# A gated cross-attention and mixture-of-experts layer on one core: the router's products on four column quarters, its running counts inside PSUM, the bias row added in place, and the steps of each group in another order

## The chip, the cores and the metric

One core of a Trainium2 chip runs the whole program in one launch. The time is the device time of one execution, in microseconds (us); lower is better. The engines are TensorE (PE, with its weight loads as PEld), VectorE (DVE), ScalarE (ACT), GpSimd (POOL) and SyncE (SP, which issues DMAs).

## What is computed

Four sequences of 1024 tokens with 256 features. The text side is normalised and attends over its context (64 rows of 192 features, masked) and over itself; the result, gated, is added to the tokens. Then each token goes to two of eight experts.

```python
x = x + tanh(g_xattn) * xattn(ctx, layernorm(x), mask)   # 4 heads of 64, keys: 64 context rows + 1024 own rows
...
    qn = rmsnorm(q, qn_g) * SCALE;  kn = rmsnorm(k, kn_g)
    attn = softmax(where(mask, qn @ kn.T, -max));  out = (attn @ v) @ Wo.T + bo
...
y = layernorm(x)
logits = y @ w_router;  probs = softmax(logits);  topk_w, topk_idx = top_k(probs, 2)
x = x + tanh(g_ffn) * sum_over_chosen(weight * (gelu(y @ w1[e] + b1[e]) @ w2[e] + b2[e]))
```

## The kernel before

**Two parts.** The first part does the attention, the second normalisation and the routing, and scatters each token's row twice (once for each chosen expert) into a table in HBM. The second part (`experts_phase`) walks over tiles of 256 rows of that table, one expert's weights at a time; it starts when all rows are scattered.

**Windows and groups.** The attention is cut into 8 windows `w` (sequence `b = w // 2`, pair of heads `w % 2`). A window has 18 units `u`, 2 query halves by 9 key tiles (8 of own rows, the ninth the context's), taken two at a time in 9 groups, `i` = 0 to 8. A group is written out by hand for each engine, as a list of steps in a fixed order:

- TensorE: `scores` of two units (K and Q, three products each for two heads), `tile_steps` (two transposes `turn_heads` of the tile projected in the group before, then `project` of the next tile), `values` of the first unit of the group before, the `mid_uses`, `values` of its second unit, `sums` (every ninth unit: the softmax's denominators), and the `late_uses`. With `i == 5` the `tile_steps` stand behind the first `values`.
- ScalarE: `probabilities` of the two units (exp from PSUM), `heads_hi`, `read_projection`, then whatever belongs to another stage: `norm_hi`, `norm_rows`, `normed_rows`, `turned_rows`, `second_rows`, `take_values`.
- VectorE: `add_probabilities` (adds the exps of nine units), `heads_lo`, `mean_squares`, `add_probabilities`, `scale_heads`, and what belongs to other stages: `quotients` (i 1 and 6), `residual`, `second_stats`, `second_variance`, `norm_lo`, `norm_stats`, `router_*`.
- GpSimd: `head_roots` (the power -1/2 for the head norms), `norm_root`, `second_root`, and the indirect DMAs of `scatter`.

A tile goes round all of them: `project` (PE), `read_projection` (ACT), `mean_squares` (DVE), `head_roots` (POOL), `scale_heads` (DVE), and `turn_heads` (PE) in the next group.

**The mid and late uses.** In an even window the projection of the sequence before (`project_out`, i 0 to 3; each of its two row tiles is two fp32 products and one product `bo_pick` by `bo_cut` that adds the bias row) and the transposes of the normed rows (`turn_rows`, i 7 and 8); in an odd window the transposes of the next sequence's normed rows (`turn_norm`, i 0 to 4), and `logits` (i 0) and `ranks` (i 4) of the sequence before. These results lie in the two PSUM banks `psF` that the projected tiles use in turn; `wait_bank_free` waits until the last user of a bank has been read. Behind the last window the same steps stand one after the other for the last sequence (`tail_uses`).

**The router.** `logits` is 16 products (8 row tiles by 2 halves of the features) of the turned rows as weights and the 128x8 router as moving data. `router_logits`, `router_softmax`, `router_largest` (twice) and `router_rows` on VectorE find the two experts; `ranks` multiplies the 0/1 matrix `chosen` by a triangular matrix and by ones; `router_slots` adds up the counts of the eight row tiles one after the other (`base`, eight small adds that wait for each other), and makes the row numbers for `scatter`.

## Time and profile before

| | us |
|---|---|
| median of 3 runs | 1027.05 (1022.74 to 1029.36) |
| profiled execution, its own time | 1023.27 |
| its span, first to last instruction | 1021.7 |
| attention, the eight windows | 43.9 to 517.4 |
| tail: last sequence's projection, norm, routing and scatter | 517.4 to 583.3 |
| experts | 583.3 to the end |
| granted TensorE clock, mean | 0.944 of full |

The profile is of one execution. A busy TensorE is an engine with an instruction in flight; at half clock it is busy too, for longer. [...]

### The profile page before, as it was taken

To read this page: it belongs to the slowest core of one execution; us is meant where nothing else is said; L and a number is where in the kernel's file an instruction comes from. 1 tells how busy PE (TensorE), PEld (TensorE's weight loads), DVE (VectorE), ACT (ScalarE), POOL (GpSimd) and SP (SyncE) were. 2 spreads that over 40 slices of the span, in tenths; PEclk is the share of its full clock that TensorE was granted. 3 is DMA by queue.
4 is the path that set the end of the run, shared out by engine and by line. 5 is a ranking of instruction groups with operands and counts; after the bars stand their busy time and mean duration, and the time that the engine had idled before them with its cause. 6 is when DMAs were issued, how large, how long until landed. Compare 5 with 4: busy or idle time off the path is not lost. (4 is left out here: it accounts for less than half of the span.)

```text
span 1021.7 us, 19903 instructions
## 1 busy us (share of the span) xinstructions
PE 890.3 (87%) x6028; PEld 682.5 (67%) x6028; DVE 625.9 (61%) x1497; ACT 544.4 (53%) x1439; POOL 351.8 (34%) x271
## 2 busy tenths in 40 slices
PE   4899989898898978989772099999999999999990
PEld 3644445454454645545342099999999999999990
DVE  5566676656766476564966156676757657757650
ACT  3777755856658566475513035454546445546430
POOL 2333232322655225552162422423323423333221
PEclk8999999998999899999995599999999999999996
DMA  4301000210002210010032342525252534342325
GB/s 124 126 1 44 2 0 20 68 40 2 32 32 67 79 42 32 32 63 1 16 110 71 107 129 41 134 45 130 44 136 41 134 46 129 54 126 42 50 32 174
DMA packets 49215, 66.31 MB, mean 65 GB/s; under 512 B 7409, under 2 KB 42993, under 8 KB 49105
## 3 DMA queue, kind: packets, MB, share of 16 engines
q0 software_dynamic: 17520, 33.27, 14.8%
q1 hardware_dynamic: 29296, 30.18, 10.0%
q10 hardware_dynamic: 2352, 2.31, 0.8%
q8 instruction: 22, 0.36, 0.1%
q14 instruction: 25, 0.20, 0.1%
HBM read 41.54 MB, written 28.39 MB: 68 GB/s over the span
## 5 line engine op out<-in xcount | busy, mean ns | idle before, releaser
L500 POOL TENSOR_TENSOR rr<-ssm,minus_half 128x4 f32<-128x4 f32 (+1 forms) x72 | 121.7, 1690 | 290.5 <-DVE ssm L791 290.5
L1615 PE MATMUL psH<-xT_hi,Q 128*128 128x256 f32 x1120 | 203.9, 281 | 1.6 <-DVE xT_lo L1532 1.6
L1628 PE MATMUL psY<-K,g_hi 128*128 128x256 f32 x1120 | 203.4, 284 | 0.0
L1468 POOL DMA_INDIRECT total<-y_out,token_i x70 | 115.0, 1643 | 255.4 <-DVE y_out L1553 243.9
L665 ACT ACTIVATE p_ring<-psS,shift 128x1024 f32<-128x1024 f32 x128 | 137.1, 1111 | 104.2 <-PE psS L1263 104.1
L1615 PEld LDWEIGHTS psH<-xT_hi,Q 128*128 128x128 f32 x1120 | 174.5, 190 | 2.0 <-issue 2.0
L1628 PEld LDWEIGHTS psY<-K,g_hi 128*128 128x128 f32 x1120 | 171.7, 188 | 0.0
L1628 PE MATMUL psY<-K,g_lo 128*128 128x256 f32 x560 | 157.3, 281 | 0.0
L1615 PE MATMUL psH<-xT_lo,Q 128*128 128x256 f32 x560 | 157.2, 281 | 0.0
L1279 PE MATMUL psO<-p_ring,V 128*64 128x512 f32 x576 | 151.5, 623 | 0.8 <-ACT o_sb L653 0.8
L827 DVE TENSOR_TENSOR p_sum<-p_sum,p_ring 128x1024 f32<-128x1024 f32 (+1 forms) x112 | 136.5, 1219 | 2.2 <-ACT p_ring L665 1.4
L1502 ACT ACTIVATE g<-psH,b_col 128x256 f32<-128x256 f32 x280 | 113.8, 474 | 29.6 <-DVE g_lo L1569 28.0
L1502 ACT ACT_TABLE_LOAD x35 | 44.9, 1283 | 158.8 <-PE psH L1615 158.7
L1263 PE MATMUL psS<-Q,K 64*128 64x512 f32 x864 | 126.8, 427 | 0.5 <-ACT p_ring L665 0.5
L1263 PEld LDWEIGHTS psS<-Q,K 64*128 64x128 f32 x864 | 79.9, 195 | 63.6 <-issue 44.1
L1567 DVE CAST g_hi<-g 128x512 fp32r<-128x512 f32 x140 | 62.7, 448 | 77.1 <-ACT g L1502 77.1
L1615 PEld LDWEIGHTS psH<-xT_lo,Q 128*128 128x128 f32 x560 | 106.2, 190 | 0.0
L1628 PEld LDWEIGHTS psY<-K,g_lo 128*128 128x128 f32 x560 | 105.7, 189 | 0.0
L1569 DVE TENSOR_TENSOR g_lo<-g,g_hi 128x512 fp32r<-128x512 f32 x140 | 96.9, 692 | 4.8
L508 POOL DMA_INDIRECT routed<-big,slot_i x64 | 72.1, 1127 | 57.7 <-ACT big L615 20.6
L1547 DVE TENSOR_TENSOR y<-psY,b_row 128x256 f32<-128x256 f32 x70 | 29.0, 423 | 56.7 <-PE psY L1628 56.7
L1279 PEld LDWEIGHTS psO<-p_ring,V 128*64 128x64 f32 x576 | 32.0, 138 | 46.4 <-issue 38.2
(238 smaller groups left out, 1248.7 us busy)
## 6 DMA issues: line engine op xcount, KB each, us to landing
lnf<-routed SPq DMA_DIRECT2D x35, 258.0 KB
xr<-in_L_ffn_w POOLq DMA_DIRECT2D x7, 1024.0 KB, 6.3
xn<-in_L_ffn_w POOLq DMA_DIRECT2D x7, 1024.0 KB, 8.7
xr<-in_x SPq DMA_DIRECT2D x8, 512.0 KB, 4.8
xb<-in_x SPq DMA_DIRECT2D x4, 1024.0 KB, 6.2
total<-xb SPq DMA_DIRECT2D x4, 1024.0 KB, 4.5
routed<-pad_rows SPq DMA_DIRECT2D x8, 258.0 KB, 4.4
total<-y_out,token_i POOLq DMA_INDIRECT x70, 3.9
```

The costliest lines, as they stand in the source:

```text
L500: pool.tensor_tensor(rr[0:p, c % 2, n], ssm[0:p, c % 2, n], minus_half[0:p, n], ALU.pow).then_inc(rr_ready, 1)
L508: pool.indirect_dma_start(routed, bass.IndirectOffsetOnAxis(ap=slot_i[:, k, t:t + 1], axis=0), rows[k][:, t, :], None, bounds_check=NE * R ...
L665: act.activation(p_ring[0:p, u % RING, :], psS[u % 2][0:p].rearrange("p a n -> p (a n)"), ACT.Exp, bias=bias).then_inc(exp_done, 1)
L827: dve.tensor_tensor(total, p_ring[0:p, (u - 1) % RING, :] if k == 1 else total, p_ring[0:p, u % RING, :], ALU.add).then_inc(p_added, 1)
L1263: ins = pe.matmul(psS[u % 2][:, odd, :], kk[rows_of, f, keys], qq[rows_of, f, cols], start=(m == 0), stop=(m == len(products) - 1))
L1279: ins = pe.matmul(psO[0][head, :], V[:, (w % 2) * KT + kt, head], p_ring[:, u % RING, odd * HALF:(odd + 1) * HALF], start=(kt == 0), stop= ...
L1468: pool.indirect_dma_start(total, bass.IndirectOffsetOnAxis(ap=token_i[:, m:m + 1], axis=0), y_out[:, m, :], None, bounds_check=NTOK + TM - ...
L1502: act.activation(g32[:, q % 2, (c % 2) * TM:(c % 2 + 1) * TM], psH[q][:, (c % 2) * TM:(c % 2 + 1) * TM], ACT.Gelu_apprx_tanh, bias=b1_col[ ...
L1567: dve.tensor_copy(g_hi[:, 2 * q:2 * q + 2, :], g).then_inc(g_hi_ready, 1)
L1569: dve.tensor_tensor(g_lo[:, 2 * q:2 * q + 2, :], g, g_hi[:, 2 * q:2 * q + 2, :].bitcast(F32), ALU.subtract).then_inc(g_ready, 1)
L1615: ins = pe.matmul(o, l, r, start=(n == 0), stop=(n == len(parts) - 1))
L1628: ins = pe.matmul(psY[m][:, 0:D], l[:, c, cols], r[:, c, :], start=(c == 0 and n == 0), stop=(c == HC - 1 and n == 2))
```

## The change

- `router` becomes 32 columns wide (8 used, the rest zero) and is the weights of `logits`: for each half of the features, four products, each on a quarter of the array's columns, over 256 of the 1024 turned rows. The result (`lgT`, experts in partitions) is copied to SBUF by ScalarE (`take_logits`) and turned back by two transposes (`turn_logits`, use `lt`); VectorE reads the logits from there.
- `ranks` is one product with the triangular matrix over 72 columns and eight with the ones, over 64, 56, ... 8 columns, added in PSUM, so that each tile's prefix comes out of PSUM; `router_slots` needs one add for the slots and one for `base`, which begins at each expert's region.
- The bias row is no longer a product: `tbo`, the gated bias, is added to the residual rows in place (`residual_base`, two adds of 128x1024 in groups 7 and 8 of each even window).
- TensorE does both `values` and the `sums` before the mid uses. `turn_rows`' odd uses and two of the `lt` go to the bank of the sums (bank 7); the tail uses spread over six banks.
- Steps of other stages move: `logits` to i 1 (i 0 in the last window), `lt` one later, `ranks` to i 6 (i 4 in the last), the router's steps on VectorE and ScalarE with them; `norm_lo` ahead of `quotients`; `second_offsets` behind `scale_heads`; `norm_stats` and `norm_variance` into the odd window, `norm_root` to its group 8; `scatter` to i 7 and 8 of the odd window and i 0 to 5 of the even one (from i 6, and i 0 to 4), in the last window from i 5.

```diff
@@ uses of the banks
+                if w % 2 == 1 and b >= 1:
+                    last = b + 1 == B
+                    if i == (0 if last else 1):
+                        return [("logits", b - 1)]
+                    if i == (1 if last else 2):
+                        return [("lt", b - 1)]
+                    if i == (4 if last else 6):
+                        return [("ranks", b - 1)]
...
+                        apart = name[0] == "turn" or name[0] == "lt" and name[1] + 2 < B
+                        yield 7 if apart else g % 2, name
@@ GpSimd
-                        if b + 1 < B and i == (4 if b == 0 else 1):
-                            norm_root(b + 1)
+                        if b == 0 and i == 4:
+                            norm_root(1)
                         if b >= 1 and i == 5:
                             second_root(b - 1)
-                        if b >= 2 and i < 5:
-                            scatter(b - 2, 6 + 2 * i, 2)
+                        if b >= 2 and i < 6:
+                            scatter(b - 2, 4 + 2 * i, 2)
...
+                    if w % 2 == 1 and i == 8 and b + 2 < B:
+                        norm_root(b + 2)
@@ ScalarE
+                def take_logits(b):
+                    name = ("logits", b)
+                    act.wait_ge(logits_done, b + 1)
+                    act.activation(lgT[:], bank(name)[:, 0:2 * P], ACT.Copy).then_inc(bank_read[bank_of[name]], 1)
...
-                        first = 5 if b == 0 else 2
+                        first = 5 if b == 0 else 1
                         if first <= i < first + 4:
                             norm_rows(b + 1, 2 * (i - first), 2)
@@ VectorE
+                def residual_base(b, half):
+                    dve.wait_ge(xb_loaded[b % 2], b // 2 * 16 + 16)
...
+                    dve.tensor_tensor(xb[:, b % 2, t, :], xb[:, b % 2, t, :], tbo[:].unsqueeze(1).to_broadcast([P, HT, D]),
+                                      ALU.add).then_inc(xb_ready, 1)
...
-                    for t in range(T):
-                        dve.tensor_tensor(base[:, t + 1, :], base[:, t, :], bank(name)[:, D + t * NE:D + (t + 1) * NE],
-                                          ALU.add).then_inc(base_ready, 1)
-                        dve.wait_ge(base_ready, b * (T + 2) + (t + 1))
...
+                    then_step(dve.tensor_tensor(slot[:], bank(name)[:, 0:T * NE].rearrange("p (t e) -> p t e", t=T),
+                                                base[:].unsqueeze(1).to_broadcast([P, T, NE]), ALU.add))
+                    dve.tensor_tensor(base[:], base[:], bank(name)[:, T * NE:(T + 1) * NE],
                                       ALU.add).then_inc(bank_read[bank_of[name]], 1)
...
+                    if not even and past and i == (5 if last else 7):
+                        router_slots(b - 1)
+                    if not even and past and last and i == 3:
+                        router_softmax(b - 1)
+                    if not even and past and last and i == 4:
+                        router_largest(b - 1, 1)
+                        router_rows(b - 1)
...
+                    if not even and more and i < 5:
+                        norm_lo(b + 1, i)
+                    if even and past and i == 6:
+                        second_offsets(b - 1)
...
+                    if even and i in (7, 8):
+                        residual_base(b, i - 7)
...
+                        if i in ((2, 3) if b == 0 else (0, 2)):
+                            norm_stats(b + 2, i - 2 if b == 0 else i // 2)
+                        if i == 8:
+                            norm_variance(b + 2)
...
+                        if i == 4:
+                            router_softmax(b - 1)
+                            router_largest(b - 1, 0)
+                        if i == 5:
+                            router_largest(b - 1, 1)
                             router_rows(b - 1)
@@ TensorE
-                    for t in range(T):
-                        ins = passes(bank(name)[:, t * NE:(t + 1) * NE], [(yT[:, c, t * P:(t + 1) * P], router[:, c, :]) for c in range(EC)])
+                    for c in range(EC):
+                        for j in range(4):
+                            ins = pe.matmul(bank(name)[j * BLOCK:(j + 1) * BLOCK, 0:2 * P], router[:, c, :],
+                                            yT[:, c, j * 2 * P:(j + 1) * 2 * P], start=(c == 0), stop=(c == EC - 1))
...
-                    pe.matmul(bank(name)[:, 0:T * NE], tri[:], chosen[:], start=True, stop=True)
-                    pe.matmul(bank(name)[:, D:D + T * NE], ones[:], chosen[:], start=True, stop=True).then_inc(rank_done, 1)
+                    pe.matmul(bank(name)[:, 0:(T + 1) * NE], tri[:], chosen[:], start=True, stop=False)
+                    for t in range(T):
+                        behind = bank(name)[:, (t + 1) * NE:(T + 1) * NE].rearrange("p (t e) -> p t e", e=NE)
+                        ins = pe.matmul(behind, ones[:], chosen[:, t * NE:(t + 1) * NE].unsqueeze(1).to_broadcast([P, T - t, NE]),
+                                        start=False, stop=(t == T - 1))
...
-                                     + [(bo_pick[:], bo_cut[:])])
...
                         values(2 * g - 2)
+                        values(2 * g - 1)
                     if i == 5:
                         tile_steps(g)
+                    if g >= 1:
+                        for u in (2 * g - 2, 2 * g - 1):
+                            sums(u)
                     for name in mid_uses(w, i):
                         use(name)
-                    if g >= 1:
-                        values(2 * g - 1)
-                        for u in (2 * g - 2, 2 * g - 1):
-                            sums(u)
```

## Rows read from the trace of the kernel before

**Rows 1.** The page: TensorE's busy time, and its granted clock in 40 slices

```profile
PE 890.3 (87%) x6028; PEld 682.5 (67%) x6028; DVE 625.9 (61%) x1497; ACT 544.4 (53%) x1439; POOL 351.8 (34%) x271
...
PEclk8999999998999899999995599999999999999996
```

**Rows 2.** Busy time by stretch: windows 1, 3, 6, 7, tail, experts

```profile
core 0: us, PE busy (x) PEld busy (x) DVE busy (x) ACT busy (x) POOL busy (x), PEclk, DMA share, GB/s
...
88.50:145.00 56.50, 50.92 (x279) 26.57 (x279) 37.53 (x73) 39.73 (x127) 16.63 (x10) 0.97 0.07 20
...
208.30:274.70 66.40, 57.74 (x313) 32.12 (x311) 42.47 (x106) 42.10 (x129) 19.97 (x13) 0.92 0.03 9
...
404.40:468.10 63.70, 59.95 (x317) 32.61 (x317) 39.45 (x87) 38.65 (x126) 32.88 (x23) 1.00 0.12 42
468.10:517.40 49.30, 43.18 (x241) 22.01 (x241) 34.80 (x72) 24.91 (x42) 13.58 (x10) 0.93 0.05 19
517.40:583.30 65.90, 20.61 (x96) 14.68 (x92) 29.45 (x102) 8.92 (x12) 27.69 (x26) 0.64 0.34 103
583.30:1000.50 417.20, 413.28 (x3500) 412.72 (x3500) 266.35 (x596) 204.14 (x386) 134.63 (x97) 0.99 0.38 80
```

**Rows 3.** Waits of TensorE, 40 to 520 us (total, times, longest)

```profile
PE psF L1206 <- DVE qkd L801: 16.5, 16, 1.9
PE psF L1232 <- DVE chosen L929: 10.1, 3, 4.3
PE psF L1160 <- DVE ln_lo L786: 5.0, 3, 1.9
PE psF L1216 <- DVE K L812: 4.4, 3, 1.5
```

**Rows 4.** Timeline of TensorE, window 3: logits and the scores behind

```profile
214.23 3.74 PE L1160 MATMUL psF<-router,yT 128*128 128x8 f32 x32
217.90 2.57 PE L1263 MATMUL psS<-Q,K 64*128 64x512 f32 x12
```

**Rows 5.** Timeline of TensorE, window 4, group 0: the projection's products

```profile
278.78 1.13 PE L1160 MATMUL psF<-wo,att 128*128 128x256 f32 x4
279.84 0.38 PE L1160 MATMUL psF<-bo_cut,bo_pick 64*128 64x256 f32 x1
280.15 1.13 PE L1160 MATMUL psF<-wo,att 128*128 128x256 f32 x4
```

**Rows 6.** Timeline of TensorE, window 2, group 6: both value steps together

```profile
190.07 1.94 PE L1279 MATMUL psO<-p_ring,V 128*64 128x512 f32 x8
...
191.94 1.65 PE L1263 MATMUL psS<-Q,K 64*128 64x512 f32 x12
```

**Rows 7.** Timeline of window 2, groups 5 to 7: roots, offsets, next transposes

```profile
186.69 1.01 POOL L500 TENSOR_TENSOR rr<-ssm,minus_half 128x4 f32<-128x4 f32 x1 [3.62 <-DVE ssm L791]
...
188.99 2.55 POOL L495 TENSOR_TENSOR rstd<-var,minus_half 128x8 f32<-128x8 f32 x1 [1.29 <-DVE var L870]
...
191.77 2.08 ACT L609 ACTIVATE big<-xb,off,rstd 128x256 f32<-128x256 f32 x4 [0.17 <-DVE off L762]
...
192.35 1.91 POOL L500 TENSOR_TENSOR rr<-ssm,minus_half 128x4 f32<-128x4 f32 x1 [0.81 <-DVE ssm L791]
...
194.78 0.44 PE L1206 MATMUL psF<-ident,qkd 128*128 128x128 f32 x2 [1.19 <-DVE qkd L801]
```

**Rows 8.** GpSimd's indirect DMAs: ns shortest/median/longest

```profile
L508 POOL DMA_INDIRECT routed<-big,slot_i x64: 970/1024/1967, 263.3 to 575.1; - x64
```

**Rows 9.** VectorE's adds of 128x1024 by form, 30 to 530 us

```profile
L827 DVE TENSOR_TENSOR p_sum<-p_sum,p_ring 128x1024 f32<-128x1024 f32 x96 | 117.1, 1220 | 2.1 <-ACT p_ring L665 1.4
```

**Rows 10.** Timeline of the tail: logits, counts, last scatter

```profile
539.98 4.58 PE L1160 MATMUL psF<-router,yT 128*128 128x8 f32 x32 [0.78 <-ACT yT L641]
...
550.06 1.53 DVE L945 TENSOR_TENSOR base<-base,psF 128x8 f32<-128x8 f32 x8
...
575.10 0.97 POOL L508 DMA_INDIRECT routed<-big,slot_i  x1 [0.30 <-issue]
```

More of the change, by code:

```diff
@@ L1050, in _ @@
                         quotients(2 * w)
-                    if even and past and i < 4:
-                        residual(b - 1, i)
-                    if not even and more and i < 5:
-                        norm_lo(b + 1, i)
-                    if even and past and i == 5:
-                        second_variance(b - 1)
-                    if even and more:
-                        if i == 0 and b >= 1:
-                            norm_variance(b + 1)
-                        if i == 7:
-                            mask_to_bias(b + 1)
+                    if even and past:
+                        if i < 4:
+                            residual(b - 1, i)
+                        if 2 <= i < 6:
+                            second_stats(b - 1, i - 2)
+                        if i == 5:
+                            second_variance(b - 1)
+                    if even and i in (7, 8):
+                        residual_base(b, i - 7)
+                    if even and more and i == 7:
+                        mask_to_bias(b + 1)
                     if w == 0 and i in (1, 2):
@@ L1238, in project_out @@
                     pe.wait_ge(att_ready, b * 4 + (3 if q < 2 else 4))
[L1239 to L1240 removed]
                     for n in range(2):
                         t = 2 * q + n
[L1243 to L1244 removed]
+                        ins = passes(bank(name)[:, n * D:(n + 1) * D], [(att[:, c, t * P:(t + 1) * P], wo[:, c, :]) for c in range(EC)])
                     ins.then_inc(o_done, 1)
@@ L1288, in sums @@
                     pe.wait_ge(p_added, (j + 1) * (SUMS - 1))
-                    if j == 0:
-                        wait_bank_read(pe, ("tile", 5))
-                    if kt == SUMS - 1 and j > 0:
-                        pe.wait_ge(den_taken, u // KT)
+                    wait_bank_free(pe, ("sums", j))
                     for odd in range(2):
@@ L1298, in use @@
                 def use(name):
-                    kind = {"wo": turn_output_weights, "norm": turn_norm, "out": project_out, "turn": turn_rows, "logits": logits, "ranks": ranks}[name[0]]
+                    kind = {"wo": turn_output_weights, "norm": turn_norm, "out": project_out, "turn": turn_rows, "logits": logits, "lt": turn_logits,
+                            "ranks": ranks}[name[0]]
                     kind(*name[1:])
```

163 lines of the change are left out of this document (86 added, 77 removed).

## The prediction

> **What bounds the kernel now.** The page comes first: TensorE is busy for 890.3 of 1021.7 us, VectorE for 61%, the others less [rows 1]. So the question in each stage is why TensorE is not at work, or at work slowly. The view by stretch splits this [rows 2]. The experts (417 us) are TensorE work without gaps; nothing of the change touches them. The attention is 473.5 us: in window 3 TensorE is busy 57.74 of 66.40 us, 8.7 idle, in window 6 59.95 of 63.70, in window 7 43.18 of 49.30; windows 2 and 4 are like 6 (3.4 and 4.3 idle) and 5 like 3 (7.8). The tail (65.9 us) is a chain through all engines with TensorE busy a third of it.
>
> The granted clock is the second loss. [...] The timeline shows what went before: the twelve score products behind the logits take 2.57 us against 1.65 [rows 4, 6]. Behind 32 products of 8 columns the engine runs at half clock though it was never idle; other such stretches follow waits of 1.8 us and more.
>
> The waits say what the idle time is [rows 3]: 16.5 us for VectorE's `scale_heads` (the loop of a tile through ACT, DVE, POOL, DVE, which needs about 7.2 us from a group's first score to the next `turn_heads`, as long as a plain group of 4.9 us with the 1.6 us of scores behind it, and a little more), 10.1 for `chosen` ahead of `ranks`, 5.0 for `ln_lo`, 4.4 for a bank ahead of `turn_rows`.
>
> **The bias row.** In `project_out` the bo product adds 280.15 - 279.84 = 0.31 us to each row tile [rows 5]. 24 of them lie in the attention: -7.4 us; 8 in the tail, where TensorE sets the pace: -2.5. Part is given back: in group 1 of an even window VectorE does `quotients` (2.35 us) ahead of `residual`, and the project of group 2 needs that bank. Today the residual ends just in time; TensorE arriving 1.1 us sooner waits 1.1, three times, +3.3. The replacement is eight adds of 128x1024, 1.22 us each [rows 9], in groups 7 and 8 of even windows. VectorE has the room there on average; each pushes the next `mean_squares` some 0.7 us where the loop is tight. I take +0.5 for window 0 and have the rest in the sums by window below; without cover it is 9.8 us.
>
> **The logits.** 32 instructions take 217.90 - 214.23 = 3.67 us in window 3 [rows 4]. The new form is 16 instructions of 256 columns. No row has products on a quarter of the columns; the bounds are from the nearest. The projection, on all columns, takes 1.06 us for four instructions of 256 columns [rows 5], 4.2 for 16. The values, on halves of the columns, take 191.94 - 190.07 = 1.87 us for eight of 512 [rows 6]; for 16 of 256 that is 1.9, and if the quarters overlapped four deep it would be 0.9. I take 1.8, since the order on the engine (the two passes of one product, then of its neighbour) is that of the values. With two transposes (0.3) the sum is -1.6 for each sequence, -4.8 in the attention. [...]
>
> `ranks` grows from two small products to nine, about 0.06 to 0.1 us each: +0.5 a sequence, +1.5 in the attention.
>
> **Both value steps together.** Eight value instructions take 1.87 us together and about 2.05 when a mid use splits them, as the second column half of each step overlaps only with a value step. 34 groups have a mid use: 34 x 0.15 = -5 us. The mid use also comes 0.9 us later in its group, so the small bank waits (0.4 and 0.1) in the projections go.
>
> **The waits, window by window.** I followed each engine's list through a group with the durations of the trace (exps 2.0, heads 0.55, reads of a projection 1.05, a norm's pair on ACT 1.45, an add 1.14 pace, POOL's root 1.92).
> - Windows 3 and 5: the `ln_lo` wait (1.8, 1.2) goes, as `norm_lo` now stands ahead of `quotients`; the wait for `chosen` (2.9) with the bank wait before it (1.1) goes, as `ranks` stands two groups later. In their place: `logits` now stands directly behind `turn_norm` in the same bank and waits for ACT's two reads, 1.5. `router_softmax` and `router_largest` (3.8 us with `router_rows`) fall into groups 4 and 5, `quotients` into 6, `router_slots` to the top of 7: VectorE gets behind, `mean_squares` is late by 1 us in group 5, 1.6 in 6 and 2.8 in 7. And `project` of group 7 wants the bank that `router_slots` frees: 2.5 to 3 us of waiting there. I get 8.2 us of idle time for each, against 8.7 and 7.8: nothing gained, but the work is 1.85 less (logits, ranks, values).
> - Windows 4 and 6: this is where I expect a loss. `second_variance` now comes behind `scale_heads` in group 5 and is 2 us later; GpSimd then does `second_root` (2.55) [rows 7], two scatters that used not to stand there (2 x (1.02 + 0.3) = 2.6 [rows 8]), and only then group 6's `head_roots`. `turn_heads` of group 7 waited 1.19 [rows 7] and will wait about 4.3. `second_offsets` stands behind that `scale_heads`, so ACT's `normed_rows` (2.08, begun at 191.77 before) and the exps behind it are late too: 2.1 us for the bank of `turn_rows`. Idle time 9.0 against 4: +5.0 each, less 3.4 of work.
> - Window 2 has no scatter: +3.0 idle, -3.4 work.
> - Window 1: +1.0 idle, -0.7 work, `norm_lo` and `quotients` only change places.
> - Window 7: the wait for `chosen` (4.35) shrinks to at most 1, some others go with it: -4.6 idle, -1.1 work.
>
> [...] This trace has both cases: the same root takes 1.01 us beside VectorE's idle or one-input time and 1.91 beside its adds [rows 7]. `residual_base` is such an instruction. It stands behind the root of its own group, so I charge nothing for it; beside every root it would cost 0.9 us a time, 7 us in all for the eight.
>
> **The clock.** Of nine stretches at the lower level eight lie behind the logits, `ranks` and `ln_lo`. Those go: -5.3 in window 3 and in 5, -3.5 in 7, 14 us. Five new waits of 2.5 us and more arise (groups 7 of windows 2 to 6); I give three of them a stretch of 1.7: +5.
>
> **Sum of the attention.** Window 0 +0.5, 1 +0.3, 2 -0.4, 3 -7.6, 4 +1.6, 5 -6.8, 6 +1.6, 7 -9.2, new low stretches +5: -15.0.
>
> **The tail.** bo -2.5. Logits take 4.58 us [rows 10], and VectorE copies them at once; now 1.8 to 2.5 for the products, then a copy on ACT (0.4), two transposes (0.3 to 0.4), hops of 0.2, about 3.0: -1.6. The counts: 1.53 us of eight adds [rows 10] and three small steps go, ranks adds 0.8: -1.0. Six banks instead of two: -0.2. Behind it 16 scatters (to 575.10 [rows 10]) run as before. -5.3.
>
> Together -20.3: 1023.27 - 20.3 = 1003.0 for a profiled run. The median before lies 3.8 above the profiled time; I put the median after at **1005**.
>
> **The rivals.** (a) The waits do not come as I followed them: ACT and VectorE have slack that I did not see, windows 4 and 6 gain their 3.4 us of work, the new stretches at half clock stay out: -15.0 - 2 x 4 - 5 - 4 (windows 3, 5) = -32, with the tail -37: 990. For it: each new wait is an estimate over six hops. Against: the loop's slack in the trace is 0.06 us in most plain groups.
> (b) The column quarters do not overlap: 4.2 us instead of 1.8, four times, +9.6, and the engine's clock falls behind them as before, +1.7 each, +6.8: 1021. Against: the values do overlap. This is the case in which the change does not do what it says.
> (c) The stretches at half clock only move: every one of five new waits brings one, and the small products of `ranks` and `lt` another in windows 3, 5, 7: +8.5 on top: 1013.
> (d) Slower: GpSimd's queue becomes the bound. With two scatters a group needs 1.95 + 2 x (1.02 + 0.3) = 4.6 us, a plain group has 4.9. At the longest scatter of the trace (1.97) [rows 8] it is 6.5: 1.6 us more in groups 4 and 5 of the even and 7 and 8 of the odd windows, 1.9 more in group 6, 8.3 a sequence, twice, 17, and half clock behind each of ten such waits, 17: 1005 + 34 = 1039. It begins to outweigh the gain when the mean passes about 1.7 us. Against: the median is 1.02.
>
> **How the numbers follow.** The forecast 0.50, (a) 0.20, (b) 0.10, (c) 0.14, (d) 0.06. A change under 1% (10 us) can't be told from none here. Forecast, (a) and (c) are faster by more than that, but for the near end of their spread: faster 0.81, same 0.13, slower 0.06. The range reaches from (a) at 990 to (c) and the near side of (b), 1017: 990 to 1017.
>
> **What would show it.** Right: no L1160 with `bo_cut`; the 16 logits instructions within 1.6 to 2.2 us and full clock behind them; the waits for `chosen` and `ln_lo` gone from TensorE's list; a wait of about 4 us of `turn_heads` in group 7 of windows 4 and 6 and about 2 in window 2; windows 3 and 5 near 59 us, 4 and 6 near 65 to 67, 7 near 40, the tail 60.5. Wrong: window 3 or 5 above 63 us (VectorE's router steps are then worse than I followed), logits above 3 us, or GpSimd without a gap through an even window.

## The result, and the profile after

The changed kernel takes 1010.15 us (median of 4 runs, 1007.38 to 1011.21) beside 1024.89 for the kernel before in the same session (4 runs): ratio 0.985, 95% interval 0.980 to 0.990, so the gain is real and under 2%. Its profiled execution took 1010.11 us, span 1008.5, against 1023.27. So 13 to 15 us are gained; the forecast was 1005 beside a median of 1027.05, 22 us.

The view by stretch, cut at the same events as [rows 2] (the start of each window's first exp, the last products of the sums, the first transposes of the experts): windows 0 to 7, the tail, the experts.

```profile
core 0: us, PE busy (x) PEld busy (x) DVE busy (x) ACT busy (x) POOL busy (x), PEclk, DMA share, GB/s
42.20:90.60 48.40, 41.51 (x236) 21.85 (x234) 29.79 (x68) 34.40 (x104) 13.52 (x8) 1.00 0.00 1
90.60:147.30 56.70, 49.03 (x279) 26.26 (x279) 38.37 (x74) 39.27 (x126) 16.23 (x10) 1.00 0.06 20
147.30:211.00 63.70, 57.33 (x309) 32.90 (x309) 41.70 (x103) 42.81 (x135) 20.31 (x12) 0.97 0.15 47
211.00:273.60 62.60, 53.26 (x306) 28.43 (x306) 43.96 (x102) 41.20 (x131) 17.48 (x11) 0.95 0.03 10
273.60:339.10 65.50, 57.37 (x309) 32.86 (x307) 41.20 (x101) 42.70 (x135) 35.59 (x26) 0.97 0.20 70
339.10:401.00 61.90, 53.59 (x306) 29.05 (x306) 41.50 (x93) 41.25 (x130) 17.69 (x12) 0.94 0.09 30
401.00:467.00 66.00, 58.51 (x311) 33.11 (x309) 40.19 (x86) 38.38 (x127) 33.42 (x25) 0.95 0.13 45
467.00:511.50 44.50, 39.94 (x234) 17.99 (x232) 34.98 (x65) 25.11 (x43) 15.46 (x12) 0.96 0.07 24
511.50:569.50 58.00, 14.90 (x81) 10.81 (x77) 27.86 (x94) 9.30 (x13) 25.72 (x25) 0.60 0.39 115
569.50:1008.50 439.00, 414.04 (x3500) 413.48 (x3500) 266.84 (x596) 203.99 (x386) 138.61 (x98) 0.97 0.40 87
```

Beside [rows 2]: window 3 went from 66.4 to 62.6 us, window 7 from 49.3 to 44.5, the tail from 65.9 to 58.0, but window 6 from 63.7 to 66.0. There the idle time grew from 3.75 to 7.5 us. The attention as a whole took 511.5 - 42.2 = 469.3 us beside 473.5, the tail 7.9 less, what lies ahead of the attention 1.7 less, the experts 0.6 more: 13.2 us of span. The start can't be credited to the change: a_mid below has the same steps ahead of the attention and begins it at 43.9 like the kernel before, a_product at 40.7.

The clock column says what became of the second loss: one minus the clock, times the length, is 1.9 + 3.1 + 2.0 + 3.7 + 3.3 + 1.8 = 15.8 us over windows 2 to 7. The kernel before lost 15.8, too, by the same product: 0.08 x 66.4 = 5.3 in window 3 [rows 2], as much in 5 (339.0 to 404.4, clock 0.92), 1.7 in 1 and 3.5 in 7. Its low stretches are at half clock: the record reads 0.50 from 219 to 221 us. The low clock was in the odd windows alone and is now in the even ones as well; it has not become less. (Cut in pieces of half a us, the sums are 15.3 before and 15.3 after, nine stretches of about 1.7 us lost each.) The record and the slow matmuls fall together in the trace: in window 3 of the kernel before the slow ones run from 217.9 to 221.8, and the record is at 0.59 and 0.56 in 218 to 220 and 220 to 222 and at 1.00 on either side, so a loss stands in the window in which it arose.

The two losses can be told apart over the whole attention. TensorE is idle for 58.8 us (42.9 before), 15.9 more, where the forecast's terms come to some 9 more; it is busy for 410.6 (430.7), 20 less at the same loss to the clock. The work went as the change meant it to, and the waits took most of it back.

TensorE's waits, 40 to 510 us (total, times, longest), the answer to [rows 3]:

```profile
PE psF L1251 <- DVE qkd L832: 21.4, 29, 3.3
PE psO L1335 <- ACT o_sb L678: 9.7, 8, 1.5
PE psO L1347 <- DVE p_sum L858: 5.1, 7, 1.0
PE psF L1205 <- DVE base L988: 4.6, 2, 2.3
PE psF L1205 <- DVE xb L893: 4.1, 3, 1.4
PE psF L1271 <- ACT ln_hi L602: 3.1, 2, 1.5
...
PE psF L1287 <- DVE chosen L971: 2.8, 1, 2.8
...
PE psF L1205 <- DVE ln_lo L817: 0.6, 1, 0.6
```

`chosen` fell from 10.1 to 2.8 and `ln_lo` from 5.0 to 0.6, but the second and third rows are waits that the kernel before hardly had and the prediction did not name. The second is TensorE's second value step in group 5, in all eight windows; the 0.8 us of window 7 was there before, 8.9 are new. Timeline of window 4, group 5 (start, duration, engine, line), all from the kernel after:

```profile
309.14 2.12 ACT L690 ACTIVATE p_ring<-psS,shift 128x1024 f32<-128x1024 f32 x2 [0.36 <-PE psS L1319]
309.72 1.08 PE L1335 MATMUL psO<-p_ring,V 128*64 128x512 f32 x4
...
311.15 0.60 ACT L678 ACTIVATE o_sb<-psO 128x512 f32<-128x512 f32 x1
...
311.89 1.08 PE L1335 MATMUL psO<-p_ring,V 128*64 128x512 f32 x4 [1.09 <-ACT o_sb L678]
```

In group 5 the first value step (309.72) ends a sum, ACT must copy it (`take_values`) and the second step starts a new sum in the same bank. ACT does two exps first and reaches the copy at 311.15. In the order of before the projection stood between the two value steps and covered exactly this; now it stands behind both, and TensorE is idle for 1.09 us.

### The profile page after: what moved, and what is told of

Same layout as the page of the kernel before. It is cut to its first block and busy times, and to the rows that moved or that the text cites. A ratio compares the mean times of both kernels' runs of the same rounds, so it can differ in the third digit from the quotient of the medians.

```text
span 1008.5 us, 19761 instructions
## 1 busy us (share of the span) xinstructions
PE 862.8 (86%) x5968; PEld 666.2 (66%) x5968; DVE 629.7 (62%) x1470; ACT 541.8 (54%) x1443; POOL 348.3 (35%) x269
## 5 line engine op out<-in xcount | busy, mean ns | idle before, releaser
L517 POOL TENSOR_TENSOR rr<-ssm,minus_half 128x4 f32<-128x4 f32 (+1 forms) x72 | 117.3, 1630 | 286.0 <-DVE ssm L822 286.0
L1335 PE MATMUL psO<-p_ring,V 128*64 128x512 f32 x576 | 145.9, 624 | 9.7 <-ACT o_sb L678 9.7
L1319 PE MATMUL psS<-Q,K 64*128 64x512 f32 x864 | 123.1, 416 | 0.6 <-ACT p_ring L690 0.5
L1335 PEld LDWEIGHTS psO<-p_ring,V 128*64 128x64 f32 x576 | 35.6, 140 | 75.4 <-issue 49.1
L832 DVE TENSOR_TENSOR qkd<-psF,rr 128x256 f32<-128x256 f32 (+1 forms) x65 | 26.6, 410 | 63.6 <-POOL rr L517 63.6
```

The costliest lines, as they stand in the source:

```text
L517: pool.tensor_tensor(rr[0:p, c % 2, n], ssm[0:p, c % 2, n], minus_half[0:p, n], ALU.pow).then_inc(rr_ready, 1)
L1319: ins = pe.matmul(psS[u % 2][:, odd, :], kk[rows_of, f, keys], qq[rows_of, f, cols], start=(m == 0), stop=(m == len(products) - 1))
L1335: ins = pe.matmul(psO[0][head, :], V[:, (w % 2) * KT + kt, head], p_ring[:, u % RING, odd * HALF:(odd + 1) * HALF], start=(kt == 0), stop= ...
```

## The experiments

**The second value step of group 5.** The kernel after, with that one step behind the projection again:

```diff
                     if g >= 1:
                         values(2 * g - 2)
-                        values(2 * g - 1)
+                        if i != 5:
+                            values(2 * g - 1)
                     if i == 5:
                         tile_steps(g)
+                        values(2 * g - 1)
```

> The changed kernel with the second value step of group 5 put back behind tile_steps (all else as changed). Theory: the wait of TensorE for o_sb in group 5 (1.09 to 1.51 us, eight windows, 9.7 us in all) goes, turn_heads of group 6 comes sooner too; -5 to -9 us, and in windows 4 and 6 less, since GpSimd's queue sets turn_heads of group 7 there. Rival: the loop through the head norms has this slack anyway and the idle time turns up in groups 6 and 7: less than 2 us.

994.84 us, ratio to before 0.968 (0.962 to 0.974): 15 us less than the kernel after, more than either theory gave. The wait is 0.8 us in all, TensorE's idle time in the attention falls by 8.4 us (58.8 to 50.3), and the clock's loss (same sum, all windows) is 10.6 instead of 15.8 us: 9.2 in windows 2 to 7 and 1.4 in window 0, which had none. Of the 14.0 us by which the attention is shorter the waits are thus the larger part, and the clock is nearly all of the rest.

**Scatters out of GpSimd's way.** The kernel after, scattering 3, 3, 2, 2, 2 in groups 0 to 4 of the even windows instead of 2 in each of groups 0 to 5 (b 2 and 3 only, so windows 4 and 6):

```diff
-                        if b >= 2 and i < 6:
-                            scatter(b - 2, 4 + 2 * i, 2)
+                        if b >= 2 and i < 5:
+                            scatter(b - 2, (4, 7, 10, 12, 14)[i], 3 if i < 2 else 2)
```

> The changed kernel with no scatter in group 5 of the even windows (three each in groups 0 and 1 instead of two). Theory (the forecast's step for windows 4 and 6): turn_heads of group 7 waits 3.27 us there for GpSimd, which does two indirect DMAs between second_root and head_roots; without them it waits 0.7 as in window 2, normed_rows comes sooner, and windows 4 and 6 lose 2 to 2.6 us each and the stretch at half clock behind the wait (1.7): -4 to -8 in all. Rival: ScalarE's normed_rows behind second_offsets sets the pace by itself, and the windows change by less than 1 us.

1002.27 us, ratio 0.975 (0.969 to 0.981), 8 us less than after. Window 4, groups 5 to 7, of the kernel after shows what was paid for. `second_root` runs 2.48 us, the two scatters stand behind it, then the root of the heads, VectorE's product, and TensorE's transposes 3.27 us late:

```profile
319.00 2.48 POOL L512 TENSOR_TENSOR rstd<-var,minus_half 128x8 f32<-128x8 f32 x1 [2.15 <-DVE var L910]
...
321.66 1.04 POOL L525 DMA_INDIRECT routed<-big,slot_i  x1 [0.18 <-issue]
323.01 0.98 POOL L525 DMA_INDIRECT routed<-big,slot_i  x1 [0.30 <-issue]
324.01 1.05 POOL L517 TENSOR_TENSOR rr<-ssm,minus_half 128x4 f32<-128x4 f32 x1
325.09 0.42 DVE L832 TENSOR_TENSOR qkd<-psF,rr 128x256 f32<-128x256 f32 x1 [3.44 <-POOL rr L517]
...
325.57 0.63 PE L1251 MATMUL psF<-ident,qkd 128*128 128x128 f32 x2 [3.27 <-DVE qkd L832]
```

Without the two scatters it takes 8.72 us instead of 11.28 from the exps of group 6 to those of group 7, in windows 4 and 6. That is not a net gain of 5.1. The waits for `qkd` fall from 21.4 to 16.2 us, but the wait of `turn_rows` for its bank, which they had covered, rises from 2.1 to 5.5: TensorE's idle time falls by 1.8 us only (58.8 to 56.9). The clock's loss falls by 5.3 (15.8 to 10.5), one stretch less in window 5 and two in 6. By window 4, 5 and 6 are 1.4, 1.7 and 2.9 us shorter, 6.0 of the 7.9. So the gain is for the larger part the clock's, and the rival, that ScalarE's `normed_rows` sets the pace, is right for a part of the waits.

**The bias row alone, and the order alone**, each put into the kernel before. The first takes the `bo` product out of `project_out` and adds `tbo` to `xb` on VectorE; the second is only

```diff
                     if g >= 1:
                         values(2 * g - 2)
+                        values(2 * g - 1)
                     if i == 5:
                         tile_steps(g)
-                    for name in mid_uses(w, i):
-                        use(name)
                     if g >= 1:
-                        values(2 * g - 1)
                         for u in (2 * g - 2, 2 * g - 1):
                             sums(u)
+                    for name in mid_uses(w, i):
+                        use(name)
```

> The kernel before with only the bias row changed: no product of bo, tbo added in place in groups 7 and 8 of even windows. Theory (the timeline of after: 16 projection instructions at 0.22 us each against 1.37 us for a row tile of five before): each bias product costs 0.48 us, not 0.31, so TensorE's work falls by 11.5 us in the attention and 3.8 in the tail. In the attention most of it is lost again in waits (residual behind quotients ahead of the project of group 2, 1.1 to 1.4 a sequence; the bank wait in groups 0 to 3), so the attention gains 4 to 7 us and the tail 3.8; in all -8 to -11. Rival: the eight adds of 1.22 us delay the head norms' loop by about as much as the products cost, and the attention gains nothing; in all -4.

1018.5 us, ratio 0.989 (0.983 to 0.996), in a session in which the kernel before took 1029.79. By the ratio this part alone gives 1.1%, with an interval from 0.4 to 1.7%, so it can't be set against the whole change's 1.5%. The profiled execution says where it went. In windows 2, 4 and 6, where the products lay, TensorE is busy 9.6 us less and idle 2.1 more, 7.5 shorter in all, and from the tail's first product to the transposes it is 3.9 less: near the theory's 4 to 7 and 3.8. But windows 1, 3, 5 and 7, which never had such a product, are 6.1 us longer together, with 22 us lost to the clock in them instead of 15.8, and the attention as a whole is 0.8 us shorter. The products cost about what the theory says, and low clock elsewhere took most of it back.

> The kernel before with only TensorE's order changed: both value steps and the sums ahead of the mid uses. Theory: the value step of the window's second half (unit 9) now stands ahead of tile_steps in group 5 and waits for ScalarE's copy of the first half's result (take_values behind two exps), 1.1 to 1.5 us in each of eight windows where before it was covered by the transposes and the projection; that eats the 5 us that joined value steps give and the bank waits that they cover: within 3 us of before. Rival (as forecast): -5 us of work and -2 of bank waits, -6 to -8 in all.

1054.4 us, ratio 1.023 (1.016 to 1.030): slower, by far more than any theory allowed. The attention is 25.3 us longer (498.8 beside 473.5), TensorE's idle time in it 23.3 (66.2 beside 42.9). The new order on VectorE's steps of before has the wait for `take_values` (7.5 us), `ln_lo` at 6.4 instead of 5.0, `p_sum` 6.2, two waits that were not there (`turn_rows` for ScalarE's `yT` 4.1, the projection for `xb` 2.3), and the `logits` directly behind `turn_norm`. Window 3, group 0 shows that last one; [rows 4] has the same products of the kernel before:

```profile
222.04 1.08 PE L1294 MATMUL psO<-p_sum,ones 128*64 128x512 f32 x4 [0.97 <-DVE p_sum L827]
223.05 0.66 PE L1171 MATMUL psF<-ident,xn 128*128 128x128 f32 x4
225.24 4.12 PE L1160 MATMUL psF<-router,yT 128*128 128x8 f32 x32 [1.54 <-ACT ln_hi L582]
229.29 2.93 PE L1263 MATMUL psS<-Q,K 64*128 64x512 f32 x12
```

**The same with group 5 repaired**: b_order, with the second value step of group 5 behind the projection.

> The kernel before with the new order of TensorE, but the second value step of step 5 behind the projection. The new order alone made the kernel before 2.3% slower (some 1050 beside 1027). If the wait for the taken values at step 5 (9.7 us in all with the clock stretches that follow it) is the larger part of that, this one comes to 1030 to 1035, ratio 1.005. If the other waits that the new order lengthened on the old VectorE order (ln_lo 2.80, 1.37 and 2.25 at step 2, chosen 3.9) carry it, it stays over 1042, ratio above 1.015.

1035.06 us, ratio 1.009 (1.006 to 1.013). By the ratios the repair gives back 1.4%, 14 us; what is left is still slower than the kernel before. Its attention is 14.5 us longer than before and its idle time 13.5, and the place is windows 3 and 5: 72.1 and 71.0 us beside 66.4 and 65.4, at a clock of 0.88 beside 0.92. In window 3 the 32 products of the logits take 6.2 us behind that wait of 1.54, beside 3.7 in [rows 4].

**The old order in the kernel after**, second value step behind projection and mid uses in all groups (the last diff backwards):

> The kernel after with TensorE's order of the kernel before in all steps: the second value step behind the projection and behind the products for other stages (everything else of the change kept). With the value step put back in step 5 alone the kernel took 0.968 of before. If that step was all that the new order cost, this one gives the same, 992 to 998. If the new order is worse in every step (the wait for p_sum at step 0 of seven windows, 0.65 to 0.96 each, goes too), 988 to 992. If it is worth something elsewhere, as the change supposes (products whose operand is late stand behind both value steps), the waits for chosen, ln_hi and the turned rows come back longer: over 1000.

999.43 us, ratio 0.975 (0.972 to 0.978): by the ratios 1.0% better than after, 0.7% worse than a_values (whose interval it overlaps). By window (lengths read as above) it is not one sign: windows 1, 3, 5 take 55.0, 57.7 and 57.5 us beside a_values' 55.1, 61.6 and 58.9, windows 2, 4, 6 take 63.4, 67.1 and 66.5 beside 60.9, 63.8 and 63.8. Apart from group 5 the new order is thus better by some 3 us in each of windows 2, 4 and 6 and by 1.4 in 7, and worse by 0 to 4 in 1, 3 and 5. In windows 4 and 6 this is the clock and not the waits: a_mid is idle no longer there (6.5 and 5.9 us beside 6.5 and 8.3), but loses 5.4 and 5.3 us to the clock beside 1.9 and 0. In window 4 the 3.14 us behind the scatters come in both; here a wait of 1.72 for the bank of `turn_rows` follows within the low stretch, and half clock lasts from 317 to 327.

**The slots of windows 3 and 5 one group earlier**, ahead of `quotients` in group 6:

```diff
-                    if not even and past and i == (5 if last else 7):
+                    if not even and past and last and i == 5:
                         router_slots(b - 1)
...
+                    if not even and past and not last and i == 6:
+                        router_slots(b - 1)
```

> The kernel after, with one thing moved: in windows 3 and 5 the slots are computed by VectorE at step 6, ahead of the quotients, and no longer at the top of step 7. In the kernel after, the projection of step 7 stands 2.28 us behind that chain (wait for base) in each of the two windows, and the TensorE clock is low right behind it (mean 0.7 and 0.8 over step 7, which takes 10.75 and 9.59 us beside 6.5 in window 1). If the wait is what brings the low clock, both go: the wait falls to under 0.7 us, step 7 of windows 3 and 5 to some 7.5 us, and the kernel gains 4 to 6 us (some 1005). If the low clock comes from something else in that step (the 8-column products of the ranks in the step before), only the waits go: 2 to 3 us (some 1007.5), clock still low. If the moved chain is late for its own reason at step 6 (chosen and ranks have not come), the wait moves to the quotients and the gain is nothing.

1005.39 us, ratio 0.980 (0.977 to 0.984), 5 us less than after, though the two intervals overlap. The wait of 2.28 us for `base` in group 7 is gone, as expected (0.54 for `qkd` ahead of it stays), but 2.47 us of waiting for `qkd` appeared in group 8, since all that VectorE does in group 6 is now later. It takes the low clock with it: 0.81 over group 8 in both windows. So this gain is not that of the wait: windows 3 and 5 shorten by 0.8 and 1.3 us only, window 2 by 1.0, because a stretch of low clock is missing in it. TensorE's idle time is 1.9 us more than after (60.6), the clock's loss 6.8 us less (9.0).

**Work in place of idle time.** In the kernel after, 10 products without use (identity by `wo`, into the bank of the sums, overwritten later) ahead of the projection of group 7 in windows 3 and 5:

```diff
+                    if w in (3, 5) and i == 7:
+                        wait_bank_read(pe, ("sums", 2 * w))
+                        for n in range(10):
+                            pe.matmul(psO[1][:, 0:D], ident[:], wo[:, 0, :], start=True, stop=True)
                     if i != 5:
                         tile_steps(g)
```

> The kernel after, with 10 products without use (identity by an output weight, 256 columns, into the bank of the sums, some 2.2 us) ahead of the projection's step 7 in windows 3 and 5, where TensorE otherwise stands 2.28 us behind VectorE's chain of slots (2.83 us idle over the step). The step's work is not shortened: if idle time of TensorE is what brings the low clock behind it (mean 0.7 and 0.8 over the step, 10.75 and 9.59 us long), the clock stays at 1.0, the step takes 7.3 to 7.8 us and the kernel gains 3 to 5 us for work added (1005 to 1007). If the low clock there has another cause (the 8-column products of step 6, or something that isn't TensorE's), the step stays at 9.5 us or more and the kernel is the same or 0 to 3 us longer.

1007.97 us, ratio 0.986 (0.984 to 0.989). Timeline of TensorE, window 3, group 7, first the kernel after:

```profile
261.87 0.69 PE L1205 MATMUL psF<-w_hi,ln_hi 128*128 128x384 f32 x1 [2.28 <-DVE base L988]
...
264.09 3.68 PE L1335 MATMUL psO<-p_ring,V 128*64 128x512 f32 x8
```

and with the useless products:

```profile
259.70 4.58 PE L1387 MATMUL psO<-wo,ident 128*128 128x256 f32 x20 [1.17 <-DVE den L865]
264.13 0.38 PE L1251 MATMUL psF<-ident,qkd 128*128 128x128 f32 x2
...
265.49 1.94 PE L1335 MATMUL psO<-p_ring,V 128*64 128x512 f32 x8
```

I had the size of the fill wrong: the ten products are twenty instructions and take 4.58 us, not 2.2. Still, from its scores to the next group's, the group of window 3 is 10.47 us long against 10.74 without them, since the eight value instructions take 1.94 us instead of 3.68. In window 5 it is 10.47 against 9.59, as the low stretch there was shorter (2.52 us for the values), and by whole windows the two are 0.3 and 1.4 us longer. So 9.2 us of useless work cost 1.7 where they stand, and nothing in the time of the kernel that is clear of noise. The mean clock over the two groups is 1.00 and 1.00 with the products and 0.68 and 0.82 without. Here idle time of TensorE ahead is what brings the clock down. But a wait makes the stretch likely, not certain: 2.47 us in group 8 are followed by half clock in both windows of a_slots and in window 5 of a_best (the group takes 9.0 us), and by full clock in window 3 of a_best (7.39). In a_best2, further down, it is half clock both times (8.8 and 9.0).

**The router products, quarter by quarter.** The kernel after with the two loops of `logits` exchanged (`for j` outside, `for c` inside):

> The kernel after, with the 16 router products in the other order of loops: the two products of one column quarter stand behind each other, and the four quarters one after the other (same products, same sums). In the kernel after, where neighbours go to different quarters, the 16 took 1.94 us, 0.12 each, beside 0.22 for a 256-column fp32 product in a row of its kind. If neighbours in different quarters overlap, the 16 take 2.9 to 3.5 us here, and each of the four sequences, the tail above all, becomes up to 1.6 us longer (1010 to 1016). If quarters never overlap and the 1.94 us come from the 32 rows of the weights alone, it stays 1.94.

1007.79 us (two runs), ratio 0.985 (0.982 to 0.987): no change that can be told from the kernel after. The 1.94 us in the expectation is from the tail, at half clock (0.50 from 530 to 532 us). In window 3, at full clock (1.00), kernel after:

```profile
224.86 1.07 PE L1271 MATMUL psF<-yT,router 128*32 128x256 f32 x16 [1.54 <-ACT ln_hi L602]
225.86 1.65 PE L1319 MATMUL psS<-Q,K 64*128 64x512 f32 x12
```

and with the loops exchanged:

```profile
223.38 1.09 PE L1271 MATMUL psF<-yT,router 128*32 128x256 f32 x16 [1.54 <-ACT ln_hi L602]
224.41 1.66 PE L1319 MATMUL psS<-Q,K 64*128 64x512 f32 x12
```

1.00 and 1.03 us from the first product to the scores. 16 instructions on all columns would be 4.2 by [rows 5], so these are four times as fast, and it does not matter whether the neighbour goes to another quarter or not. That leaves two readings which no run here tells apart: the quarters overlap in either order, or a product on 32 weight columns is quick by itself.

**A product of the old shape back.** The kernel after with one more product in each row tile of `project_out` (weights by zeros, 64 rows, fp32 replicated, 256 columns):

```diff
-    [(att[:, c, t * P:(t + 1) * P], wo[:, c, :]) for c in range(EC)]
+    [(att[:, c, t * P:(t + 1) * P], wo[:, c, :]) for c in range(EC)]
+    + [(w_hi[0:2 * BLOCK, 0, 0:P], lc_hi[0:2 * BLOCK, 0, SC:P].unsqueeze(1).to_broadcast([2 * BLOCK, 4, P - SC]))]
```

> The kernel after, with one more product in each of the 32 groups that project the output (a slice of the weights by zeros, 64 rows deep, fp32 replicated, 256 columns: the shape of the product with the bias row that the change took out; VectorE still adds the bias row too). If the product costs what its row in the trace of before shows, 0.31 us, 24 of them cost 7.4 us in the attention and 8 in the tail 2.5, less what fills the wait at step 2 of the even windows (1.4 us in each of three): some 1016. If it costs what a row tile became cheaper by in the kernel after (0.48 us), it is 11.5 and 3.8, less 4: some 1021.5. If the gain of the removed products was not theirs but that of the clock, the steps come out 0.3 to 0.5 us longer for each product and low-clock stretches come or go beside them by chance: anything from 1008 to 1025 with the steps 0 to 3 of the even windows each 0.9 us longer.

1015.49 us, ratio 0.991 (0.988 to 0.993): 5.3 us more than after, which is the 1016 of the smaller size. The sum hides several terms, though. Window 4, group 3 of this kernel:

```profile
303.48 1.13 PE L1205 MATMUL psF<-wo,att 128*128 128x256 f32 x4
304.54 0.38 PE L1205 MATMUL psF<-lc_hi,w_hi 64*128 64x256 f32 x1
304.85 1.13 PE L1205 MATMUL psF<-wo,att 128*128 128x256 f32 x4
305.91 0.38 PE L1205 MATMUL psF<-lc_hi,w_hi 64*128 64x256 f32 x1
305.92 1.75 PE L1320 MATMUL psS<-Q,K 64*128 64x512 f32 x12
```

and of the kernel after:

```profile
301.33 1.99 PE L1205 MATMUL psF<-wo,att 128*128 128x256 f32 x8
303.25 1.67 PE L1319 MATMUL psS<-Q,K 64*128 64x512 f32 x12
```

A row tile that is followed by another takes 304.85 - 303.48 = 1.37 us with the product. Eight instructions without it take 1.92, 0.96 a tile. Ahead of the scores the product costs only 0.01, as they start while it runs. The two tiles of a group cost 305.92 - 303.48 = 2.44 against 1.92; from its scores to the next group's a group is 0.60 us longer (groups 0, 1, 3 of windows 2, 4, 6: nine times, 5.4 us), and in group 2 the wait for `xb` falls from 1.4 to 0.8 and takes all of it. In the tail the eight cost 3.9. That makes 9.3, and it comes out as 5.3 (4.4 between the spans of the profiled executions) because other things moved: windows 5 and 7 are 2.6 us shorter with less low clock, the router products of the tail run at full clock (1.07 us beside 1.94), and the attention begins 1.5 us sooner.

**The repairs together.** a_values, a_scatter and a_slots in one kernel:

> The kernel after with three repairs at once: the second value step of step 5 behind the projection again, no scatter in step 5 of the even windows, and the slots of windows 3 and 5 at step 6. The first alone gave 0.968 of before, the second 0.975, the kernel after 0.985. Adding the gains (15.3 and 7.9 us beside after) and 4 us for the third gives 983 us; if the low clock was counted twice (both single repairs took away the same stretches: low clock 30.6 us after, 23.8 and 20.4 with each), it gives only the waits: 9.7 + 5 + 3 and half of the low clock, about 988. Over 992 would say that the repairs take the place of each other.

986.69 us, ratio 0.963 (0.960 to 0.966), 2.2% less than after by the ratios, near the 988 in which the low clock is not counted twice. The even windows take 60.9, 61.0 and 60.9 us. Then with the old order in the odd windows besides, as a_mid suggested:

> The kernel with the three repairs (0.9631 of before), and in the odd windows the second value step behind the products for other stages again. With that order everywhere the odd windows 1, 3, 5 took 55.0, 57.7 and 57.5 us beside 55.1, 60.1 and 59.0 with the three repairs, the even ones 63.4 to 67.1 beside 60.8. If the two kinds of window can be had apart, windows 3 and 5 come to 57.5 and the kernel to 983 (0.959 to 0.961). If the gain in the odd windows was paid by the even ones (work that is late moves over the border), the sum stays, 986 to 988.

986.13 us, ratio 0.964 (0.962 to 0.966). Windows 3 and 5 are shorter (59.0 and 57.8 beside 60.1 and 59.0), but the two kernels cannot be told apart: the spans of the profiled executions differ by 3.4 us, the medians by 0.6. Either is over 3% below the kernel before, clear of the interval, and some 2% below the kernel after by the ratios.

## Why the prediction was near, step by step

**The sum is near because only part of it failed.** The attention gained 4.2 us instead of 15.0, the tail 7.9 instead of 5.3, and 1.7 us ahead of the attention were not forecast. Of the 13.2 us of span 2.7 are not the change's (these 1.7, and one slow scatter less in the tail), so beside the forecast's 20.3 stand 10.5. That the median came within 5 us of 1005 is in part luck.

**The clock is the step that failed.** "Those go: -5.3 in window 3 and in 5, -3.5 in 7, 14 us", less 5 for new ones. The old stretches went, and as much came back at other waits: 15.8 us lost in both kernels, where 14 - 5 = 9 were to be gained. That is rival (c), the stretches only move; its 1013 is nearer to the result than the forecast's 1005. The reason, that idle time ahead brings a stretch, was right for group 7 of window 3 (a_fill); the number of new waits was too small, since the next step missed seven.

**Both value steps together, -5, came out with the wrong sign.** The work term was about right: in b_order TensorE is busy 2.0 us longer than before with 7 us more lost to the clock, so some 5 less of work, as an estimate. The waits were what failed. I counted the 0.15 us that a split value step loses (1.87 us for the two together [rows 6], 1.01 each apart in window 3 of the kernel before, from 222.07 and 223.67), and not what stands between the two in group 5: the projection, which covers ACT's `take_values`. It is 9.7 us of waiting, 8.9 of them new, and by a_values 5.2 of clock. In the kernel before the value steps waited 0.8 us for `o_sb` in all: what stood between them was cover enough. Window 0 shows the same, +3.8 us (48.4 beside 44.6) where +0.5 was put, and 46.7 in a_values, 1.4 of them clock. With it the wait for `p_sum` at group 0 rose (1.0 before, 5.1 after). With both, the order costs 1.0% on the other parts of the change (a_mid against after) and 2.3% alone (b_order).

**Windows 4 and 6** went the way that was forecast. Forecast: `turn_heads` 4.3 us late in group 7, windows 65 to 67. Measured 3.27 and 65.5, 66.0; 2.1 for the bank of `turn_rows`, measured 0.27 and none: the forecast added this wait to that of `turn_heads`, while in the trace the one covers the other (a_scatter has 1.8 in each, with the first gone). In the trace 1.05 us of root instead of 1.92 is the difference in the first. The root that ran at 324.01 met an idle VectorE and took 1.05 us, beside 1.91 in [rows 7], where VectorE's add of 192.18 (`p_sum` and `p_ring`, 1.22 us) ran next to it.

**Windows 3 and 5**, forecast near 59, took 62.6 and 61.9. The wait of `logits` is 1.54 (1.5 expected), that of the projection of group 7 is 2.28 (2.5 to 3). The excess is mostly `take_values` (1.51 each) and the clock (3.1 and 3.7 us lost, where the 5.3 of each were to vanish and 1.7 each for three new waits were charged apart).

**Window 7**, forecast near 40, took 44.5. `chosen` was to wait at most 1 us and waits 2.84: why VectorE is late there was not followed to its end.

**The logits** were sized at 1.8 us and take 1.00 at full clock. The step that failed is the choice of the values row (1.87 us for eight of 512 columns) over the fourfold end of the bounds, 0.9, which the trace comes within 0.1 us of. That interleaving the quarters is what does it, a_quarters does not bear out (1.03 us with the loops exchanged). The 4.2 us of rival (b) did not come, nor half clock behind them (the scores take 1.65); whether the quarters overlap, which is what it doubts, stays open. In the tail the engine is at half clock (0.50) and they take 1.94.

**The bias product** was put at 0.31 us each: -7.4 in the attention with 3.3 given back, -2.5 in the tail. In the attention a_product puts it at 0.30 us a tile in groups 0, 1 and 3, and at nothing in group 2, 5.4 us in all, where -7.4 + 3.3 = -4.1 was forecast: about right. In the kernel before, where the product stands ahead of a value step, b_bias gives 7.5. In the tail the tiles follow each other, so 0.48: from the first product to the transposes 17.10 us before, 525.71 - 512.50 = 13.21 after, -3.9.

**The tail, in sum.** Timeline of the kernel after:

```profile
512.50 3.72 PE L1205 MATMUL psF<-wo,att 128*128 128x256 f32 x16
...
525.71 3.65 PE L1261 MATMUL psS<-ident,big 128*128 128x128 f32 x16 [6.04 <-DVE big L918]
...
530.14 1.94 PE L1271 MATMUL psF<-yT,router 128*32 128x256 f32 x16 [0.78 <-ACT yT L661]
...
533.36 0.23 DVE L940 COPY lg<-psF 128x64 f32<-128x64 f32 x1 [6.50 <-PE psF L1280]
...
538.48 0.45 PE L1290 MATMUL psF<-chosen,ones 128*128 128x64 bf16 x8
...
540.93 1.04 POOL L525 DMA_INDIRECT routed<-big,slot_i  x1 [16.79 <-DVE slot_i L993]
...
561.17 0.97 POOL L525 DMA_INDIRECT routed<-big,slot_i  x1 [0.30 <-issue]
```

Transposes to the copy of the logits 7.65 us (9.14 before): -1.5, as expected (-1.6). Copy to first scatter 7.57 (9.25): -1.7 against -1.2. The 16 scatters 21.2 (22.2): -1.0, because one of them took 1.96 us instead of two; that is not the change's. `ranks` is 0.45 us for eight products, as put.

**What stays open.** Why one wait is followed by half clock and the next of the same length is not; and why the router products run four times as fast in either order of loops. The products of `ranks` as a cause of low clock were not tried by themselves. b_order's slowness is explained in parts only: group 5 is 14 us of it by the ratios, the remaining 0.9% lie in windows 3 and 5 and were not divided between the waits there and the clock.

## What to carry to other kernels

Before two steps of an engine are joined, look at what stands between them and at who uses that time: a block that lies between the end and the start of a sum in one bank covers the other engine's copy (1.09 to 1.51 us a window here), and a wait near zero in the trace before says how thin the cover is. Where the clock drops behind waits, a change that removes some waits and adds others is to be charged by the new waits, all of them counted, before the old stretches are credited. And put long queue work (scatters) where no instruction of a tight loop stands behind a long one of the same queue: moving two of them was worth 0.8% here, most of it by the clock. A part that is tried alone shows what it does to its own group only if the windows that it does not touch are looked at too: half clock came and went in those with every kernel here.

## What the runs showed of the hardware

- 16 fp32 instructions on 32 columns of weights and 256 of data took 1.00 us at full clock, and 1.03 in the other order of the quarters; 4.2 would be the pace of the full-width ones, four in 1.06 us [rows 5]. At half clock (0.50) they took 1.94.
- 9.2 us of useless products in two places lengthened their two windows by 1.7 us only, as the clock over their two groups was 1.00 and not 0.68 and 0.82: the eight value instructions behind them took 1.94 us and not 3.68 and 2.52.
- Half clock is not tied to the length of a wait alone: behind six waits of 2.46 to 2.48 us in the same group (a_slots, a_best, a_best2) it came five times and stayed out once.
- A replicated fp32 product between fp32 ones cost 0.41 us a row tile in a_product (1.37 beside 0.96) and 0.48 in a tail (3.9 us for eight), the same product just ahead of the scores almost nothing (they started 0.01 us behind its start).
